# The first neighbour aggregation of a four-layer graph network: two rows, fetched through DRAM, in place of the counts' whole low part

## The reference, cut to what matters

```python
h = jnp.maximum(_layernorm(x, axis=-1), 0.0)
agg = jax.ops.segment_sum(h[src], dst, num_segments=n)
cnt = jax.ops.segment_sum(jnp.ones((src.shape[0],), x.dtype), dst, num_segments=n)
mean_agg = agg / jnp.maximum(cnt, 1.0)[:, None]
h2 = mean_agg @ W_l.T + b_l + h @ W_r.T
mu, var = jnp.mean(h2, axis=0), jnp.var(h2, axis=0)
h2 = (h2 - mu) * jax.lax.rsqrt(var + 1e-05) * gamma + beta
x = x + jax.nn.relu(h2) + h
```

## Time and profile before

| | us |
|---|---|
| median of 3 runs | 392.02 (391.94 to 392.08) |
| the profiled execution | 392.54 |
| its span, first to last instruction | 391.0 |
| TensorE busy | 370.5 (95%), 1778 matmuls |
| TensorE loading weights, beside that | 279.4 (71%) |
| VectorE busy | 310.8 (79%) |
| ScalarE busy | 173.6 (44%) |
| GpSimd busy | 4.2 (1%) |
| share of the chain that ended last | TensorE 75%, VectorE 16%, ScalarE 5%, DMA 2% |

### The profile page before, as it was taken

How to read it: one execution, slowest core, us unless ns; L and a number is a source line. 1 busy time by engine, 2 the same in 40 slices (tenths; PEclk the granted TensorE clock), 3 DMA queues, 4 the chain that set the end, 5 groups by cost and what they waited for, 6 DMA issues and landing times.

```text
span 391.0 us, 5095 instructions
## 1 busy us (share of the span) xinstructions
PE 370.5 (95%) x1778; PEld 279.4 (71%) x1778; DVE 310.8 (79%) x657; ACT 173.6 (44%) x291; POOL 4.2 (1%) x19
## 2 busy tenths in 40 slices
PE   2879999999999999999989999999999999999994
PEld 1545566666666888887768788887678878787873
DVE  5889999999939689897886978499875778578246
ACT  4754665463136233443467723361363531125530
POOL 4000000000000000000000000000000000000000
PEclk9999999999999999999999999999999999999999
DMA  7602445343226000066400320400320023000002
GB/s 236 256 1 70 133 158 160 106 135 113 72 63 234 1 3 0 2 216 244 185 2 1 109 108 17 197 2 0 120 97 0 3 95 120 1 2 0 2 0 107
DMA packets 16360, 32.92 MB, mean 84 GB/s; under 512 B 1360, under 2 KB 1488, under 8 KB 16336
## 3 DMA queue, kind: packets, MB, share of 16 engines
q1 hardware_dynamic: 15744, 32.25, 23.8%
q10 hardware_dynamic: 592, 0.36, 0.4%
HBM read 21.07 MB, written 1.05 MB: 57 GB/s over the span
## 4 chain that ended last, share of the span: by engine, by line
PE 75%; DVE 16%; ACT 5%; issue 3%; DMA 2%; ACTq 0%; DVEq 0%
PE acc L1394 12%; PE bank L1376 10%; PE bank L1479 7%; PE bank L1268 6%; PE bank L1270 6%; PE bank L1249 4%; PE bank L1464 3%; PE acc L1249 3%; PE acc L1268 3%; PE acc L1270 3%; PE acc L1450 3%; DVE big_rounded L655 2%; PE acc L1226 2%; PE bank L1226 2%; PE acc L1544 2%
## 5 line engine op out<-in xcount | busy, mean ns | idle before, releaser
L1394 PE MATMUL acc<-wide_rounded,c_rounded 128*126 128x512 f32 x200 | 59.5, 438 | 0.7 <-ACT acc L462 0.7
L1394 PEld LDWEIGHTS acc<-wide_rounded,c_rounded 128*126 128x126 f32 x200 | 36.9, 187 | 19.7 <-issue 13.0
L795 DVE TENSOR_SCALAR wide_rounded<-iota_f,picked 128x512 fp32r<-128x512 f32 x100 | 42.2, 480 | 1.5 <-issue 1.1
L481 ACT COPY z_sb<-acc 126x512 f32<-126x512 f32 x37 | 21.6, 585 | 41.9 <-PE acc L1394 33.1
L505 ACT ACTIVATE wide<-wide,low_col 128x512 f32<-128x512 f32 x32 | 21.3, 715 | 32.9 <-DVE low_col L908 32.8
L628 DVE TENSOR_TENSOR wslot_rounded<-wslot,wide_rounded 128x512 fp32r<-128x512 f32 x24 | 16.2, 687 | 22.5 <-ACT wslot L375 22.5
L1479 PEld LDWEIGHTS bank<-v_sb,big 128*128 128x128 f32 x256 | 29.7, 192 | 4.7 <-issue 4.3
L1479 PE MATMUL bank<-v_sb,big 128*128 128x65 f32 x256 | 31.6, 277 | 0.0
L801 DVE TENSOR_TENSOR c_rounded<-row_bc,wslot_rounded 128x1008 fp32r<-128x1008 bf16 x25 | 30.0, 1200 | 0.0
L1376 PE MATMUL bank<-t_sb,wslot 128*128 128x512 f32 x64 | 29.5, 594 | 0.5 <-ACT t_sb L457 0.5
L655 DVE TENSOR_TENSOR big_rounded<-big,big_rounded 128x1024 fp32r<-128x1024 f32 x24 | 29.1, 1221 | 0.4
(11 more groups left out here) (306 smaller groups left out, 763.4 us busy)
## 6 DMA issues: line engine op xcount, KB each, us to landing
big<-z_sb SPq DMA_DIRECT2D x36, 252.0 KB
big<-in_w SPq DMA_DIRECT2D x4, 2048.0 KB, 7.8
x_sb<-in_x SPq DMA_DIRECT2D x8, 256.0 KB, 5.1
big<-in_w_3t SPq DMA_DIRECT2D x2, 1024.0 KB, 6.7
row_bc<-in_rows SPq DMA_DIRECT2D x7, 256.0 KB, 6.4
wslot<-in_wq SPq DMA_DIRECT2D x1, 1024.0 KB, 9.4
wslot<-in_wk SPq DMA_DIRECT2D x1, 1024.0 KB, 11.3
wslot<-in_wv SPq DMA_DIRECT2D x1, 1024.0 KB, 13.3
```

Of the source, the lines that this page charges most:

```text
L481: nc.scalar.copy(stage[0:BROWS, b % STAGES, :], a).then_inc(S["staged"], 1)
L795: nc.vector.tensor_scalar(hot_ring[:, u, k, :], iota_f[:, :], picked[:, 0, s0 + k:s0 + k + 1], None, ALU.is_equal)
L1394: last = nc.tensor.matmul(to, st_ring[:, u, 2 * k + a, :, :].rearrange("p w k -> p (w k)"), hot_ring[:, u, k, :], start=False, stop=False, ...
```

## The change

The counts are whole numbers. Only an entry of 4096 or more can have a low part; its row of `c1` then has a sum of 4096 or more, and with 8192 edges there are at most two such rows. The change finds these rows (where there is none, rows 0 and 511), splits them alone, and takes of the product with the counts' low parts these two rows only. The other aggregations are as before, and the split of all of `c1` on VectorE stays, since a later one reads `c1_lo`.

- ScalarE's four copies of the counts to `c1` also give the row sums, `most`.
- GpSimd makes two small tables of row numbers at the start. In unit 13 of the attention VectorE marks the rows with a sum of 4096 or more and takes the largest mark of each partition in both directions, `heavy_no` (128 x 2).
- TensorE transposes the two columns into one row of bank 7, ahead of `ff2`, and then waits behind the first bank of `ff2`, before the second, until VectorE has read them (`heavy_ready`).
- VectorE makes two row numbers of them with nine small instructions on one partition (`heavy_rows`), in its queue behind the split of `c1` and before the first residual.
- SyncE stores `c1` in DRAM behind the load of `w2_0`, loads the two numbers into registers, fetches the two rows, stores the four rounded tiles of `h1` in DRAM as they come, and fetches the same two rows of these. The load of `w1_2` now stands behind all that in its queue.
- GpSimd rounds and splits the two rows of the counts and rounds the two of `h1`.
- In the aggregation L1544's loop has 16 matmuls instead of 32, and at the end four matmuls with a contraction of two rows are added, which wait for GpSimd.

The diff, without declarations:

```diff
@@ SyncE
             load("w1_0", w1_0)
             load("w2_0", w2_0)
+            for t in range(NT):
+                sp.dma_start(counts_kept[t * P:(t + 1) * P, :], c1[:, t, :]).then_inc(S["counts_out"], 16)
             sp.wait_ge(S["ff1_mm"], FT)
             load("w_lr", wl_t, 0)
             load("w_lr", wr_t, 1)
+            sp.wait_ge(S["heavy_ready"], 1)
+            _, heavy_rows = nc.values_load_multi_w_load_instructions(heavy_i[0:1, :], engines=[mybir.EngineType.SP], ...
+            sp.wait_ge(S["counts_out"], 16 * NT)
+            for i in range(HEAVY):
+                sp.dma_start(heavy_c[i:i + 1, :], counts_kept[bass.ds(heavy_rows[i], 1), :]
+                             ).then_inc(S["heavy_c_in"], 16)
+            by, before_these, _, _ = parts["h1"]
+            for t in range(NT):
+                sp.wait_ge(S[by], before_these + t + 1)
+                sp.dma_start(highs_kept[t * P:(t + 1) * P, :], z_sb_r[:, t, :].bitcast(F32)).then_inc(S["highs_out"], 16)
+            sp.wait_ge(S["highs_out"], 16 * NT)
+            sp.wait_ge(S["heavy_parts"], 2)
+            for i in range(HEAVY):
+                sp.dma_start(heavy_c[i:i + 1, :], highs_kept[bass.ds(heavy_rows[i], 1), :]
+                             ).then_inc(S["heavy_h_in"], 16)
             sp.wait_ge(S["ff2_mm"], NT)
@@ GpSimd
+            nc.gpsimd.iota(row_no[:, 0, :], [[P, NT]], base=1, channel_multiplier=1, ...
+            nc.gpsimd.iota(row_no[:, 1, :], [[-P, NT]], base=N, channel_multiplier=-1, ...
...
+            pool.wait_ge(S["heavy_c_in"], 16 * HEAVY)
+            nc.gpsimd.tensor_copy(heavy_hi, heavy_c).then_inc(S["heavy_parts"], 1)
+            pool.wait_ge(S["heavy_parts"], 1)
+            nc.gpsimd.tensor_tensor(heavy_lo, heavy_c, heavy_hi.bitcast(F32), ALU.subtract
+                                    ).then_inc(S["heavy_parts"], 1)
+            pool.wait_ge(S["heavy_h_in"], 16 * HEAVY)
+            nc.gpsimd.tensor_copy(heavy_h, heavy_c).then_inc(S["heavy_h_ready"], 1)
@@ ScalarE, counts_out
-                nc.scalar.copy(c1[:, t, :], bank[4 + t][:, :]).then_inc(S["c1_ready"], 1)
+                nc.scalar.activation(c1[:, t, :], bank[4 + t][:, :], ACT.Copy, accum_out=most[:, t:t + 1]
+                                     ).then_inc(S["c1_ready"], 1)
@@ VectorE
+            def heavy_rows():
+                first, second = heavy_f[:, 0:1], heavy_f[:, 1:2]
+                same, other = heavy_f[:, 2:3], heavy_f[:, 3:4]
+                dve.wait_ge(S["most_turned"], 1)
+                link(nc.vector.tensor_reduce(heavy_f[:, 0:HEAVY],
+                                             bank[7][0:1, 0:HEAVY * P].rearrange("p (a n) -> p a n", a=HEAVY),
+                                             AX.X, ALU.max))
+                mark(nc.vector.tensor_scalar(first, first, -1.0, 0.0, ALU.add, ALU.max))
+                link(nc.vector.tensor_scalar(second, second, -1.0, float(N), ALU.mult, ALU.add))
+                link(nc.vector.tensor_single_scalar(second, second, float(N - 1), ALU.min))
+                mark(nc.vector.tensor_tensor(same, first, second, ALU.is_equal))
+                link(nc.vector.tensor_scalar(other, first, float(N // 2), -float(N), ALU.is_ge, ALU.mult))
+                link(nc.vector.scalar_tensor_tensor(out=other, in0=other, scalar=float(N // 2), in1=same,
+                                                    op0=ALU.add, op1=ALU.mult))
+                link(nc.vector.tensor_tensor(second, second, other, ALU.add))
+                nc.vector.tensor_copy(heavy_i[:, :], heavy_f[:, 0:HEAVY]).then_inc(S["heavy_ready"], 1)
...
                     on_diagonal(rcnt_bc, rcnt_c)
+                    dve.wait_ge(S["row_numbers"], HEAVY)
+                    link(nc.vector.scalar_tensor_tensor(
+                        out=row_no[:, :, :], in0=most[:, :].unsqueeze(1).broadcast_to([P, HEAVY, NT]),
+                        scalar=float(EXACT), in1=row_no[:, :, :], op0=ALU.is_ge, op1=ALU.mult))
+                    nc.vector.tensor_reduce(heavy_no[:, :], row_no[:, :, :], AX.X, ALU.max).then_inc(S["most_ready"], 1)
...
                                         ALU.subtract).then_inc(S["c1_parts_ready"], 1)
+            heavy_rows()
@@ TensorE, product_in_parts
                     last.then_inc(S[done], 1)
+                    if m == 0 and second_bank:
+                        pe.wait_ge(*second_bank)
@@ TensorE
             pe.wait_ge(S["ff1_ready"], NT)
+            pe.wait_ge(S["most_ready"], 1)
+            for i in range(HEAVY):
+                last = nc.tensor.transpose(bank[7][0:1, i * P:(i + 1) * P], heavy_no[:, i:i + 1], ident[:, :])
+            last.then_inc(S["most_turned"], 1)
             product_in_parts(hi, halves(wide_at, wide_lo, FT), weight("w2_0"), reads("ff_mid", FT), "ff2_mm",
-                             weight_lo="w2_0_lo")
+                             weight_lo="w2_0_lo", second_bank=(S["heavy_ready"], 1))
...
                 pe.wait_ge(*reads("h1")[k][0])
-                for i in range(2):
-                    for m in range(NT):
-                        nc.tensor.matmul(bank[m][:, :], tile(h1[k][0], m), c1s[k][i], start=(k == 0 and i == 0),
-                                         stop=False)
+                for m in range(NT):
+                    nc.tensor.matmul(bank[m][:, :], tile(h1[k][0], m), c1s[k][0], start=(k == 0), stop=False)
...
                 for m in range(NT):
-                    last = nc.tensor.matmul(bank[m][:, :], tile(h1[k][1], m), c1s[k][0], start=False,
-                                            stop=(k == NT - 1))
-                    if k == NT - 1:
-                        last.then_inc(S["agg1_mm"], 1)
+                    nc.tensor.matmul(bank[m][:, :], tile(h1[k][1], m), c1s[k][0], start=False, stop=False)
+            pe.wait_ge(S["heavy_parts"], 2)
+            pe.wait_ge(S["heavy_h_ready"], 1)
+            for m in range(NT):
+                nc.tensor.matmul(bank[m][:, :], tile(heavy_h, m), heavy_lo, start=False, stop=True
+                                 ).then_inc(S["agg1_mm"], 1)
```

More of the change, by code:

```diff
@@ L52 @@
 TINY = 1e-37
+HEAVY, EXACT = 2, 4096
+assert (HEAVY + 1) * EXACT > E
 COLS = {}
@@ L96, in gnn_kernel @@
         wslot, wslot_r = sb_rounded("wslot", [P, 4, NT, D])
-        row_bc = sb("row_bc", [P, len(ROWS), D])
+        row_bc, row_bc_r = sb_rounded("row_bc", [P, len(ROWS), D])
         col = sb("col", [P, N_COLS])
@@ L137, in gnn_kernel @@
         rcnt_sb = sb("rcnt_sb", [P, N])
+        most = sb("most", [P, NT])
+        row_no = sb("row_no", [P, HEAVY, NT])
+        heavy_no = sb("heavy_no", [P, HEAVY])
+        heavy_f = sb("heavy_f", [1, 2 * HEAVY])
+        heavy_i = sb("heavy_i", [1, HEAVY], I32)
         steps = rcnt_sb[:, 0:1 + SLOTS]
@@ L198, in gnn_kernel @@
         c2_hi = t_lo
+        heavy_c, heavy_hi = row_bc[0:HEAVY, 0, :], row_bc_r[0:HEAVY, 1, :]
+        heavy_lo, heavy_h = row_bc_r[0:HEAVY, 2, :], row_bc_r[0:HEAVY, 1, :]
+        counts_kept = nc.dram_tensor("counts_kept", (N, N), F32, kind="Internal").ap()
+        highs_kept = nc.dram_tensor("highs_kept", (N, D), F32, kind="Internal").ap()
         c2_lo = both(lambda a: a[:, 0, :, :], wslot, wslot_r)
@@ L224, in gnn_kernel @@
             "w_3_lo", "hi_scalar", "lo_vector", "wo_hi", "wo_lo", "base_ready",
-            "rcnt_ready", "dinv_ready", "c1_parts_ready", "loops_added", "c2_hi_ready", "mean_ready",
+            "rcnt_ready", "dinv_ready", "c1_parts_ready", "row_numbers", "most_ready", "most_turned", "heavy_ready", "counts_out", "highs_out",
+            "heavy_c_in", "heavy_h_in", "heavy_h_ready", "heavy_parts", "loops_added", "c2_hi_ready", "mean_ready",
             "out_done", "vector_order", "scalar_order", "pool_order", "consts", "tables",
@@ L316, in _ @@
             load("w_lr", wr_t, 1)
+            sp.wait_ge(S["heavy_ready"], 1)
+            _, heavy_rows = nc.values_load_multi_w_load_instructions(
+                heavy_i[0:1, :], engines=[mybir.EngineType.SP], min_val=0, max_val=N - 1,
+                skip_runtime_bounds_check_because="a row's number, bounded where it is made on the chip")
+            sp.wait_ge(S["counts_out"], 16 * NT)
[11 more added lines that the diff above has]
+                             ).then_inc(S["heavy_h_in"], 16)
             sp.wait_ge(S["ff2_mm"], NT)
@@ L342, in _ @@
                            allow_small_or_imprecise_dtypes=True).then_inc(S["tables"], 2)
+            nc.gpsimd.iota(row_no[:, 0, :], [[P, NT]], base=1, channel_multiplier=1,
+                           allow_small_or_imprecise_dtypes=True).then_inc(S["row_numbers"], 1)
+            nc.gpsimd.iota(row_no[:, 1, :], [[-P, NT]], base=N, channel_multiplier=-1,
+                           allow_small_or_imprecise_dtypes=True).then_inc(S["row_numbers"], 1)
             nc.gpsimd.iota(need_c[:, :], [[0, 1]], base=-NBK, channel_multiplier=1,
@@ L1235, in product_in_parts @@
```

(2 more changed lines are left out.)

## The result

The changed kernel takes 395.63 us (median; 394.2 to 397.23), the kernel before took 392.05 in the same comparison: a ratio of 1.0093 [1.0081, 1.0106], 3.6 us slower. The forecast was 394.1 in a range of 392.3 to 396.6. Most of the 1.5 us between them is one thing that the forecast had left to a rival: TensorE's clock falls in the new gap.

A forecast was written before the change was run, and what follows sets the result against it. TensorE, busy for 95% of the span, was taken as the bound. Upstream 0.65, gap 3.4, stage -1.95 and DRAM 0 gave +2.1 us on the 392.02 median: 394.1, in a range of 392.3 to 396.6.

The forecast's parts named there:

- Step 3: TensorE's wait for the row numbers before ff2's second bank: +3.4 us, between 2.9 and 4.0.
- the rival I gave 8 in 100: TensorE's clock falls in the new gap before ff2's second bank: 2 us more, 396.1; chance 0.08.
- the clock at 1.00 behind the gap: Sign of the forecast: TensorE's granted clock stays full after the wait before ff2's second bank.
- a late way through DRAM: Fetched rows come late for the four two-row matmuls: up to 1.3 us in the range; rival at 395.3, chance 0.12.
- a gap of 4.0: Upper bound of the wait before ff2's second bank, with the small VectorE instructions at 0.25 us each; 3.4 taken.
- 0.8 upstream: Amount the range's high end takes for additions ahead of ff2, which were summed at 0.65 us.
- a stage that gives back only 1.5: Low bound of the gain from first aggregation to linear product, if the waits cost more; 1.95 us taken.
- Step 1 and 2: First aggregation to linear product: matmuls -3.63 and +0.91, a new wait for ScalarE's fourth tile +0.77; net 1.95 us back.
- the bounds of the four: Two-row matmuls ending the aggregation: 0 if hidden in pipelining, 1.6 us at 0.39 each; 0.91 taken.
- The joint at the batch statistics: TensorE and VectorE tie there; VectorE comes 2.86 us earlier, TensorE 1.95, so the stage's 1.95 is kept.
- Step 4: Additions ahead of ff2: attention marks 0.3, ScalarE row sums 0.25, two transposes 0.1; sum 0.65 us.
- Step 5: Stores, fetches and GpSimd rounding for the two-row matmuls: no cost, ready 0.7 us before TensorE needs them.

The follow-up runs named there:

- the filled gap: The changed kernel with 13 unused matmuls ahead of TensorE's wait for the row numbers: 394.17 us, ratio 1.0052.
- the saving alone: The kernel before with the 16 low-part matmuls left out of the first aggregation and nothing put in their place: 389.31 us, ratio 0.9929.
- the saved matmuls put back: The changed kernel with the 16 low-part matmuls back in its aggregation, the four two-row ones staying: 398.28 us, ratio 1.0151.
- the gap alone: The kernel before with one more wait of TensorE, behind ff2's first bank for VectorE's statistics of the residual's first tile: 396.7 us, ratio 1.0102.

## Why the prediction was right, and where it wasn't

**The direction and the main step held; that the time fell into the range is in part luck.** The forecast was a wait that costs more than the saving. Step 3 put the gap at 3.4; it is 3.21, because the chain of nine small instructions took 228.97 - 227.43 = 1.54 and not 1.74 (they follow one another at 0.17 to 0.18, not 0.19). Its releaser, place and reason are as forecast, and the gap by itself makes a kernel slow that has nothing else of the change.

**The clock: the rival I gave 8 in 100.** It is in the median of the changed kernel and in its profile, at 1.6 to 1.8 us; the rival's price was 2. The sum has no term for it, and "the clock at 1.00 behind the gap", which I had named as a sign of the forecast, did not come. The 395.6 is inside the range all the same, but its upper end of 396.6 was made up of other things: a late way through DRAM (1.3), a gap of 4.0, 0.8 upstream and a stage that gives back only 1.5, of which the last alone came.

I had argued from one fall, at the end of the kernel, that it comes more than 3 us after the last matmul, and called the margin small. That fall gave the wrong kind of number: the same kernel falls or not from one execution to the next. A stand-still of 3.03 us left the clock at 1.00 in one profiled execution, and one of 1.94 brought it down in another. Nor is the gap at the end the longest at full clock in the trace before, as I wrote: its first matmul comes 5.18 us after the start, and the profile gives a clock of 1.00 over all of that. I should have put the chance near even.

The Trainium skill, TensorE: Matmul & The Clock Gate, HAM oscillation, says that after an idle gap between bursts of matmuls the next burst runs slow; it speaks of gaps somewhat longer than these. Three of the four profiled executions with a stand-still agree (the row of eight matmuls is 3.59, 3.42 and 3.11 long) and one doesn't (2.11 behind 3.03 us).

The changed kernel's execution of 394.2 and the filled gap's 394.17 are what the forecast's sum describes, 394.1. That they agree within 0.1 is better than the terms deserve: the stage is 0.43 dearer than forecast, and the gap (0.19), the steps upstream (0.07) and a stall that goes (0.31) are cheaper by about as much.

**Step 1 and 2, the stage: -1.52 for -1.95.** The wait for ScalarE's fourth tile came as worked out (E + 3.45 against E + 3.49, E being 247.19). The terms mis-sized are those after it: the four matmuls behind the wait took 1.05 and not 0.91, the 16 with the low parts 3.85 and not 3.73, and the four with two rows 1.12 and not 0.91. Against the bounds of the four (0 to 1.6) the value taken was near. Where the last part of it lies can be read from the weight loads of the changed kernel. They run ahead of their matmuls as a rule, but at the two ends of the two-row matmuls they stand for some 0.35 first and start only with their matmul (257.20 and 258.32); the kernel before has no such place in this stage:

```profile
257.19 0.76 PEld L1627 LDWEIGHTS acc<-row_bc_rounded 2*128 2x128 f32 x4 [0.35 <-issue]
258.32 0.76 PEld L1640 LDWEIGHTS bank<-t_sb_rounded,big_rounded 128*128 128x128 f32 x4 [0.36 <-issue]
```

So the extra cost seems to sit at the joints and not in the pitch of the two-row matmuls; no run tests it.

**The joint at the batch statistics** held: VectorE arrives early and waits 1.29 for TensorE, and all of the stage's gain is kept, as the saving alone shows (2.74 in the stage, 2.8 in the time).

**Step 4, upstream: +0.58 for +0.65.** Its parts are right within 0.1. What no step had is the 0.31 given back downstream, the stall that a longer VectorE program happens to lose. It hides the step in a comparison of times.

**Step 5, the way over DRAM: 0, as forecast,** and its spare is larger. The fetch of the two rows is issued at 252.68 (E + 5.49, forecast 5.5); GpSimd starts at E + 7.37 where I had the data at E + 8.3, mostly since a fetch of 2 KB lands some 0.8 us sooner than the load of the earlier trace rows that I took; rounding took 0.60 and not 0.8. Ready at 255.16, TensorE at 257.20: 2.0 to spare. ScalarE's rounding of w1_2 isn't late either: it starts at 262.13, right behind the instruction before it.

The sum with the measured terms: 0.58 + 3.21 - 1.52 + 0.07 - 0.31 = +2.0 without a fall of the clock (measured with the gap filled: +2.06), +3.8 with it (+3.6).

## What to carry to other kernels

Put a wait in TensorE's queue where the waiting buffer is first needed, not where it is convenient: every matmul behind it pays, here 3.2 us for a bank that was needed two banks later. Price a stop of TensorE such as these with and without a fall of its clock (by the times it fell in 11 of 16 executions with a gap of 3.0 to 3.2 us and in 2 of 6 with 1.9), and compare such kernels by the distribution of their executions and not by one profile. And when a consumer of some data is removed, look for work that was ordered early only for it: four subtractions of VectorE stood in front of the row numbers and of the first residual tile, and moving them gave 0.5 us.

## What the runs showed of the hardware that I had not expected

- The clock's fall isn't fixed by the length of the gap. By the times, which lie in two groups some 1.4 to 1.8 us apart in each kernel, it fell in five of six executions of the changed kernel, three of five with the saved matmuls put back, three of five of the gap alone, and two of six where only 1.94 us stood idle. The mean granted clock of each execution parts them in the same way (the changed kernel's 394.2 has 0.999, its other five 0.988 to 0.996); the fall itself is seen in three profiled ones. In these the shares add up to 3.4 us at 1.2 GHz, and it begins when matmuls are already back, by 0.3 to 0.8 us. The changed kernel's highest execution, 397.23, has the lowest clock, 0.988; it has no trace, and why it lost 1.6 more stays open.
- An instruction of VectorE can start 0.35 us late with nothing to wait for. It stands at the same place in the traces of three kernels with the same VectorE program (the one before, the saving alone, the gap alone) and is gone when two instructions are put ahead. Here that is 0.1% of the kernel, more than the whole net effect of the row sums.
- A sum of the row in ScalarE's copy to memory (0.60 and a reading instruction of 0.19) delays the next engine by some 0.1 us a copy.
